# First layer of the expert tiles in transposed form, from a per-tile copy of the expert's weights

## What is computed

```
logits = LN(x) @ router_W + router_b          # [128, 64, 8]
top1 = argmax(softmax(logits)); gate = softmax(logits)[top1]
h = relu(LN(x) @ W1[e] + b1[e])               # W1[e]: 128 x 512, e = top1
y = h @ W2[e] + b2[e]                         # W2[e]: 512 x 128
x = x + gate * y
```

## Time and profile before

| | us |
|---|---|
| median of 3 runs | 1803.63 (1802.99 to 1806.22) |
| the profiled execution, its own time | 1804.93 |
| span of its profile | 1803.2 |
| stage of the tiles, first weight load to the last instruction | 1599.5 to 1803.2 |
| of that, first to 70th `output` (69 periods) | 182.41 |

### The profile page before, as it was taken

How to read it: one execution, slowest core, us unless ns; L and a number is a source line. 1 busy time by engine, 2 the same in 40 slices (tenths; PEclk the granted TensorE clock), 3 DMA queues, 4 the chain that set the end, 5 groups by cost and what they waited for, 6 DMA issues and landing times. The chain is left out here.

```text
span 1803.2 us, 82779 instructions
## 1 busy us (share of the span) xinstructions
PE 1479.9 (82%) x34347; PEld 1289.7 (72%) x34348; DVE 1159.9 (64%) x4481; ACT 736.0 (41%) x1856; POOL 220.0 (12%) x427
## 2 busy tenths in 40 slices
PE   1547777777756999999999999999999968249997
PEld 0436666666645888888888888888888858237665
DVE  5878888888875666565656566666666658425454
ACT  2436666665643344444434343434443422013332
POOL 0000000000000000000000000000000003743333
PEclk9868988888966999999999999999999975569999
DMA  6000000000030000000000000000000036322221
GB/s 222 1 1 1 0 0 0 0 0 0 0 84 12 1 0 0 0 0 0 0 0 0 0 0 0 0 0 0 0 0 0 0 103 208 128 84 75 75 75 42
DMA packets 33458, 50.04 MB, mean 28 GB/s; under 512 B 4714, under 2 KB 24684, under 8 KB 32648
## 3 DMA queue, kind: packets, MB, share of 16 engines
q1 hardware_dynamic: 27312, 35.50, 6.7%
q0 software_dynamic: 5376, 12.66, 2.0%
q10 hardware_dynamic: 728, 1.34, 0.2%
HBM read 30.52 MB, written 19.48 MB: 28 GB/s over the span
## 5 line engine op out<-in xcount | busy, mean ns | idle before, releaser
L1554 DVE TENSOR_TENSOR hb<-psH,b_sb 128x512 f32<-128x512 f32 x72 | 49.8, 692 | 118.4 <-PE psH L1349 118.4
L891 PE MATMUL sc_a<-h_a,KH 128*128 128x48 f16 (+2 forms) x4096 | 123.9, 183 | 2.5 <-DVE h_a L1045 2.5
L891 PE MATMUL sc_b<-h_b,KH 128*128 128x48 f16 (+2 forms) x4096 | 122.9, 183 | 0.0
L851 PE MATMUL z_a<-h_a,WL 128*128 128x64 f16 x2304 | 112.5, 193 | 9.3 <-DVE h_a L1037 1.9
L851 PE MATMUL z_b<-h_b,WL 128*128 128x64 f16 x2304 | 111.9, 193 | 8.4 <-DVE h_b L1037 0.6
L931 PEld LDWEIGHTS mx_b<-pmv_b,VH 128*128 128x128 f16 x4096 | 107.1, 96 | 16.4 <-DVE pmv_b L1073 16.4
L931 PEld LDWEIGHTS mx_a<-pmv_a,VH 128*128 128x128 f16 x4096 | 107.1, 96 | 16.2 <-DVE pmv_a L1073 16.2
L931 PE MATMUL mx_b<-pmv_b,VH 128*128 128x16 f16 x4096 | 113.0, 169 | 5.4 <-DVE pmv_b L1073 0.4
L931 PE MATMUL mx_a<-pmv_a,VH 128*128 128x16 f16 x4096 | 113.0, 169 | 5.2 <-DVE pmv_a L1073 0.4
L891 PEld LDWEIGHTS sc_a<-h_a,KH 128*128 128x128 f16 x4096 | 112.8, 96 | 2.8 <-DVE h_a L1045 2.6
L466 PE MATMUL psK<-ident,xn 128*128 128x128 f32 x64 | 20.9, 327 | 113.2 <-DVE VB L671 86.6
(11 more groups left out here) (291 smaller groups left out, 3556.6 us busy)
## 6 DMA issues: line engine op xcount, KB each, us to landing
xr<-sorted_x SPq DMA_DIRECT2D x72, 129.0 KB, 2.1
XT<-in_ctxT SPq DMA_DIRECT2D x1, 4096.0 KB, 13.2
x_scratch<-X SPq DMA_DIRECT2D x1, 4096.0 KB, 15.9
TOK<-x_scratch SPq DMA_DIRECT2D x4, 1024.0 KB, 10.6
sorted_x<-zt SPq DMA_DIRECT2D x16, 129.0 KB, 6.4
w_sb<-in_w SPq DMA_DIRECT2D x1, 2048.0 KB, 10.3
b_sb<-in_b SPq DMA_DIRECT2D x1, 2048.0 KB, 21.1
out<-ys,xr POOLq DMA_INDIRECT x72, 2.3
```

The source lines that it names most:

```text
L851: mm = nc.tensor.matmul(q.z[layer][:, j * GB:(j + 1) * GB], WL[:, blk + j, w, :], mov[m], start=False, stop=False, skip_group_check=True)
L891: mm = nc.tensor.matmul(A.S[:, WIDE * n:WIDE * n + streamed(n)], KH[:, k, pair * P:(pair + 1) * P], A.h[1][:, 2 * n:2 * n + streamed(n) // ...
L1554: nc.vector.tensor_tensor(hb[:, u, :], psH[:, u, :], b1_sb[:, bass.ds(col, FF)], ALU.add).then_inc(v_hb, 1)
```

## The change

The first layer is computed transposed: `hidden` now takes blocks of 128 columns of the expert's `W1` as the stationary operand and streams `xgT` past them, so that the result is hidden units x tokens, which is what `output` needs. The transposes (`turn_hidden`) and `hb` are gone. The four blocks go two to `psH`, two to `psHT`, with a semaphore each (`p_h`, `p_h2`). As the bias is now one value per partition, bias and ReLU are one operation per block: ACT does blocks 0 and 1 from `psH`, DVE blocks 2 and 3 from `psHT`. The stationary operand is read from `w1_e`, which DVE fills per tile with a copy of the expert's 512 columns (`weights`). The bias comes from a small array `b1T`, 128 x 32, transposed on the host.

```diff
-                    def hidden(j, u, col):
+                    def hidden(j, u):
                         pe.wait_ge(a_xt, j + 1)
-                        wait(pe, v_hb, j - 1)
-                        nc.tensor.matmul(psH[:, u, :], xgT[:, u, :], w1_sb[:, bass.ds(col, FF)],
-                                         start=True, stop=True).then_inc(p_h, 1)
-
-                    def turn_hidden(j, u):
-                        ...
+                        pe.wait_ge(v_w1, j + 1)
+                        wait(pe, a_ht, 2 * (j - 1))
+                        wait(pe, v_ht, 2 * (j - 1))
+                        for c in range(FC):
+                            h = (psH, psHT)[c // 2]
+                            mm = nc.tensor.matmul(h[:, u, c % 2 * P:(c % 2 + 1) * P], w1_e[:, u, c * P:(c + 1) * P], xgT[:, u, :],
+                                                  start=True, stop=True)
+                            if c % 2 == 1:
+                                mm.then_inc((p_h, p_h2)[c // 2], 1)
 
                     def output(j, u, col):
-                        pe.wait_ge(a_ht, j + 1)
+                        pe.wait_ge(a_ht, 2 * j + 2)
+                        pe.wait_ge(v_ht, 2 * j + 2)
...
                     def step(j, u8):    # TensorE
+                        if tile(j + 2):
+                            turn(j + 2, (u8 + 2) % RING)
                         if tile(j + 1):
-                            next_col = first_column(j + 1)
+                            hidden(j + 1, 1 - u)
                         if tile(j - 1):
                             before_col = first_column(j - 1)
-                        if tile(j + 2):
-                            turn(j + 2, (u8 + 2) % RING)
-                        if tile(j):
-                            turn_hidden(j, u)
-                        if tile(j + 1):
-                            hidden(j + 1, 1 - u, next_col)
                         if tile(j - 1):
                             output(j - 1, 1 - u, before_col)
...
                     def relu(j, u):     # ACT
-                        act.wait_ge(p_ht, j + 1)
+                        col = act.value_load(etab[0:1, 2, bass.ds(j, 1)], min_val=0, max_val=(NE - 1) * FC)
                         wait(act, p_y, j - 1)
-                        nc.scalar.activation(hT[:, u, :, :].rearrange("p c n -> p (c n)"), psHT[:, u, :],
-                                             ACT.Relu).then_inc(a_ht, 1)
+                        act.wait_ge(p_h, j + 1)
+                        for c in (0, 1):
+                            nc.scalar.activation(hT[:, u, c, :], psH[:, u, c * P:(c + 1) * P], ACT.Relu,
+                                                 bias=b1_sb[:, bass.ds(col + c, 1)]).then_inc(a_ht, 1)
...
                     def step(j, u8):    # ACT
                         if tile(j + 2):
                             turned(j + 2, u)
-                        if tile(j):
-                            relu(j, u)
+                        if tile(j + 1):
+                            relu(j + 1, 1 - u)
...
-                    def add_b1(j, u):
+                    def weights(j, u):  # DVE
                         col = dve.value_load(etab[0:1, 0, bass.ds(j, 1)], min_val=0, max_val=(NE - 1) * FF)
-                        ...
+                        wait(dve, p_h2, j - 1)
+                        nc.vector.tensor_copy(w1_e[:, u, :], w1_sb[:, bass.ds(col, FF)]).then_inc(v_w1, 1)
+
+                    def relu(j, u):     # DVE
+                        col = dve.value_load(etab[0:1, 2, bass.ds(j, 1)], min_val=0, max_val=(NE - 1) * FC)
+                        wait(dve, p_y, j - 1)
+                        dve.wait_ge(p_h2, j + 1)
+                        for c in (2, 3):
+                            nc.vector.tensor_scalar(hT[:, u, c, :], psHT[:, u, (c - 2) * P:(c - 1) * P],
+                                                    b1_sb[:, bass.ds(col + c, 1)], 0.0, ALU.add, ALU.max).then_inc(v_ht, 1)
...
                     def tile_step(j, u8):   # DVE
                         u = u8 % 2
                         if tile(j + 1):
-                            add_b1(j + 1, 1 - u)
+                            relu(j + 1, 1 - u)
+                        if tile(j + 2):
+                            weights(j + 2, u)
                         if tile(j - 1):
                             add_b2(j - 1, 1 - u)
                             finish(j - 1, (u8 + RING - 1) % RING)
```

More of the change, by code:

```diff
@@ L48, in decoder_kernel @@
 def decoder_kernel(nc, x, ctxT, wqT, wkT, wvT, wi0T, wh0T, bi0, bh0, wi1T, wh1T, bi1, bh1,
-                   xwq, woT, bo, rw, rb, w1, b1, w2, b2, out):
+                   xwq, woT, bo, rw, rb, w1, b1T, w2, b2, out):
     x1_dram = nc.dram_tensor("x1_scratch", [B, T, D], F32, kind="Internal").ap()
@@ L1113, in decoder_kernel @@
             w2_sb = sb("w2_sb", [P, NE * FC * D])
-            b1_sb = sb("b1_sb", [P, NE * FF])
+            b1_sb = sb("b1_sb", [P, NE * FC])
             b2_sb = sb("b2_sb", [P, NE * D])
@@ L1144, in decoder_kernel @@
             rowf = sb("rowf", [P, NT])
-            etab = sb("etab", [P, 2, NT], I32)
+            etab = sb("etab", [P, 3, NT], I32)
             rtab = sb("rtab", [P, NT], I32)
@@ L1152, in decoder_kernel @@
             xgT = sb("xgT", [P, 2, P])
-            hb = sb("hb", [P, 2, FF])
+            w1_e = sb("w1_e", [P, 2, FF])
             hT = sb("hT", [P, 2, FC, P])
@@ L1191, in decoder_kernel @@
             p_h = sem("p_h")
-            v_hb = sem("v_hb")
-            p_ht = sem("p_ht")
+            v_ht = sem("v_ht")
+            p_h2 = sem("p_h2")
+            v_w1 = sem("v_w1")
             a_ht = sem("a_ht")
@@ L1229, in _ @@
                                    w2.rearrange("e (c p) n -> p e c n", p=P)).then_inc(s_wf, 16)
-                    sync.dma_start(b1_sb[:, :], b1.rearrange("(a e) f -> a (e f)", a=1).broadcast_to([P, NE * FF])).then_inc(s_wf, 16)
+                    sync.dma_start(b1_sb[:, :], b1T).then_inc(s_wf, 16)
                     sync.dma_start(b2_sb[:, :], b2.rearrange("(a e) f -> a (e f)", a=1).broadcast_to([P, NE * D])).then_inc(s_wf, 16)
@@ L1344, in first_column @@
                         return pe.value_load(etab[0:1, 0, bass.ds(j, 1)], min_val=0, max_val=(NE - 1) * FF)
-                    def hidden(j, u, col):
+                    def hidden(j, u):
                         pe.wait_ge(a_xt, j + 1)
-                        wait(pe, v_hb, j - 1)
-                        nc.tensor.matmul(psH[:, u, :], xgT[:, u, :], w1_sb[:, bass.ds(col, FF)],
-                                         start=True, stop=True).then_inc(p_h, 1)
-                    def turn_hidden(j, u):
-                        pe.wait_ge(v_hb, j + 1)
-                        wait(pe, a_ht, j - 1)
-                        for c in range(FC):
-                            mm = nc.tensor.transpose(psHT[:, u, c * P:(c + 1) * P], hb[:, u, c * P:(c + 1) * P], ident[:, :])
-                        mm.then_inc(p_ht, 1)
+                        pe.wait_ge(v_w1, j + 1)
+                        wait(pe, a_ht, 2 * (j - 1))
+                        wait(pe, v_ht, 2 * (j - 1))
+                        for c in range(FC):
+                            h = (psH, psHT)[c // 2]
[3 more added lines that the diff above has]
+                                mm.then_inc((p_h, p_h2)[c // 2], 1)
                     def output(j, u, col):
-                        pe.wait_ge(a_ht, j + 1)
+                        pe.wait_ge(a_ht, 2 * j + 2)
+                        pe.wait_ge(v_ht, 2 * j + 2)
                         wait(pe, v_yb, j - 1)
@@ L1368, in _ @@
                     turn(0, 0)
-                    hidden(0, 0, first_column(0))
+                    hidden(0, 0)
                     turn(1, 1)
@@ L1407, in turned @@
                         act.wait_ge(p_xt, j + 1)
-                        wait(act, p_h, j - 1)
+                        wait(act, p_h2, j - 1)
                         nc.scalar.activation(xgT[:, u, :], psX[:, u, 0:P], ACT.Copy).then_inc(a_xt, 1)
                     def relu(j, u):
-                        act.wait_ge(p_ht, j + 1)
+                        col = act.value_load(etab[0:1, 2, bass.ds(j, 1)], min_val=0, max_val=(NE - 1) * FC)
                         wait(act, p_y, j - 1)
-                        nc.scalar.activation(hT[:, u, :, :].rearrange("p c n -> p (c n)"), psHT[:, u, :],
-                                             ACT.Relu).then_inc(a_ht, 1)
+                        act.wait_ge(p_h, j + 1)
+                        for c in (0, 1):
+                            nc.scalar.activation(hT[:, u, c, :], psH[:, u, c * P:(c + 1) * P], ACT.Relu,
+                                                 bias=b1_sb[:, bass.ds(col + c, 1)]).then_inc(a_ht, 1)
                     turned(0, 0)
                     turned(1, 1)
+                    relu(0, 0)
                     def step(j, u8):
@@ L1527, in tables @@
```

(14 more changed lines are left out.)

## The result

The changed kernel takes 1972.3 us in the median of four runs (1971.6 to 1973.4) against 1804.5 us of the kernel before: a ratio of 1.093, interval 1.0911 to 1.0949. It is slower by 168 us, where 88 were forecast, and outside the range of 1842 to 1945. Experiment 4 has a further measurement of the changed kernel, with its own runs of before beside it: 1.0928 (1.091 to 1.0946).

A forecast was written before the change was run, and what follows sets the result against it. TensorE was taken to bound the kernel before; the change would close a loop whose seven terms sum to 3.93 us a period against 2.644, over 69 periods +88.7 us, giving 1892 us, range 1842 to 1945.

The forecast's parts named there:

- the loop: In the tiles, each period runs output, DVE's two ReLUs, weights copy, hidden, output in sequence: 3.93 us against 2.644.
- end to ReLU: From the end of output's last matmul to DVE's start on the ReLU: 0.14 us.
- ReLU to copy: On DVE, first ReLU to the copy's start, with a table read in the queue: 0.90 us, between 0.45 and 1.2.
- term 6: TensorE's queue reads the table between hidden and output, leaving a gap of 0.35 us, between 0 and 0.6.
- term 4: From DVE's end of the copy to TensorE's first weight load for hidden: 0.10 us, between 0.05 and 0.20.
- terms 5 and 7: TensorE's matmuls: hidden 0.96 us from first load, and output 1.05 us to the end of its last matmul.
- the clock falls: Rival: TensorE's pauses drop its clock to 1.2 GHz; 1939 us if half the periods, 1985 throughout; chance 17%.
- The shared port: Rival: DVE's copy waits for POOL's DMA issue of 0.98 us each period, giving 4.91 and 1960 us; chance 6%.
- The gain without the loop: On TensorE, removing 0.45 us of transposes a tile would gain up to 31 us if nothing else changed.
- TensorE faster: Rival: copy is in place before output ends, TensorE stays the bound, period 2.26 us, time 1777; chance 5%.
- no change: Rival: time ends within 0.2% of before, the period landing between 2.59 and 2.70 us; chance 2%.
- a sign of being wrong: Wrong if TensorE has no idle time before psH, or if ACT releases it; DVE's w1_e was expected, about 100 us.

The follow-up runs named there:

- Experiment 4: Changed kernel with four, two or one idle identity products before hidden's wait for the copy, two ReLU waits moved forward: 1.0535, 1.0523, 1.0524 against the kernel before.
- 1: Changed kernel with DVE's copy of the weights (weights(j+2)) put in front of relu(j+1): 1.0187 against the kernel before.
- 2: Changed kernel with four buffers of hT instead of two, queue order kept, so ReLU waits for output of three tiles back: 1.0162 against the kernel before.
- 6: Changed kernel, steps written out, weights copied twice 1.0531, three times 1.1162, twice with one idle product 1.0546, against the kernel before.
- experiment 5: Steps written out in place of the program's loop: changed kernel 1.0405, kernel before 0.9915, experiment 3 0.9735, each against the kernel before.
- experiment 3: Changed kernel with the weights copy in front and all four ReLU blocks on ACT: 0.9821 against the kernel before; with steps written out 0.9735, 1757.95 us.
- control: The kernel before, with its tile steps written out in place of the program's loop: 0.9915 against the kernel before.

## Why the prediction was wrong, point by point

**What bounds the kernel, and the loop: right.** TensorE was the bound. The new orders close a loop over `output`, ReLU, copy and `hidden`, at the place named. Two independent edits that open it (1, 2) take the time to within 2% of before, and the doubled copy shows up in full (6).

**The terms at 2.4 GHz: right in sum.** The forecast was 3.93 us a period and +88.7 us. With the clock held by one product, the measured difference is 0.0524 x 1805 = +95 us, and about 106 with the 0.20 us that the moved waits had saved: more than the sum, and inside its ends of +30 and +151. Term by term, forecast, then the period at 1607, then the loop (experiment 4, four products, where `output` ends at 1702.19): end to ReLU 0.14, 0.15, 0.24; ReLU to copy 0.90, 0.89, 0.98; copy 0.43, 0.43, 0.43; copy to first load 0.10, 0.06, 0.11; `hidden` with the queue's gap and `output` 2.36, 2.21, 2.27. Sums 3.93, 3.74, 4.03. The gap of term 6 was put too high: from `hidden`'s first load to `output` it was 1.00 to 1.06 us in the written-out steps, where 1.31 was forecast, and `output` itself took 1.15 for 1.05. The register work of the loop was in no term. For the changed kernel itself term 4 was 0.32 in the loop, beyond its upper end of 0.20.

**The clock: the step that failed.** "The likeliest gives 1892" took terms 5 and 7 at 2.4 GHz. The rival "the clock falls" had 17%, at 1939 if it held in half the periods and 1985 throughout. It is what happened: 56 of the 69 periods ran at 0.64 in the mean and at 5.37 us each (1655.60 to 1956.16). About 60 us of the 168 are the clock: 56 x (5.37 - 4.25), with the estimate of experiment 4. That the rival's 5.28 lies so near 5.37 is partly luck: 5.28 was worked out for a period wholly at 1.2 GHz, and two periods that were so (1676.39 to 1688.36, granted 0.51 and 0.50) took 6.22 and 5.75; the mean is lower because the clock came back in between. The chance was too small. The earlier trace rows showed one pause that was followed by a fall and one that was not, and I let that stand for a small chance, though the new kernel repeats its pause 69 times. The same trace had more to say: from 250 to 507 us TensorE pauses 24 times for 1.8 to 1.9 us, and 16 of these pauses were followed by a fall to 1.2 GHz within 2 us of their end. The Trainium skill ("TensorE: Matmul & The Clock Gate", section A second HAM failure mode: psum-queue depth-cycling), whose rule had been cited for the rival, describes a clock that goes back and forth where the engine idles between groups; the trace agrees, with 0.64 granted.

**What lets it fall** is shown in direction, not as a rule. Against the change, the clock held when the pause was made shorter by a product and the moved waits (4), and all but held when the steps were written out (5). In written-out steps it fell more often the longer the pause was: two long periods with one copy, ten with two, nearly all with three (6). The traces can be read once more for this. The table counts TensorE's pauses in the tiles that are over 1 us long and begin and end at 2.4 GHz, and those of them with a fall within 2 us of their end, in the profiled execution of each version:

| version | pauses | length, us | followed by a fall |
|---|---|---|---|
| changed kernel, written-out steps | 12 | 1.45 to 1.83 | 0 |
| changed kernel, loop | 25 | 1.64 to 2.01 | 23 |
| one product, loop | 57 | 1.24 to 1.82, all but one under 1.6 | 0 |
| all written out, one copy | 68 | 1.45 to 1.84, 64 under 1.6 | 1, after 1.82 |
| all written out, two copies | 65 | 1.80 to 2.20 | 5 |
| the same with a product | 66 | 1.61 to 2.10 | 2, after 1.98 and 2.09 |
| all written out, three copies | 23 | 2.14 to 2.16 | 23 |

No pause under 1.6 us in the tiles was followed by a fall, in these or in any other version here. The forecast took the pause as about 1.5 us, which it is in the written-out steps (1.47 mostly); in the loop it grew to 1.6 to 2.0. So the register work of the loop, small in itself, took the pause from a length that never cost the clock here to one that can. What stays open is what decides between 1.6 and 2.2 us: in the loop almost every such pause was followed by a fall, in written-out steps with two copies 5 of 65. Length alone does not explain that, and no run here shows what does.

**The shared port: rightly left out.** The copy took 427 ns in the mean of 67 (the groups by line above), never beside POOL's issue. In experiment 1, 65 of the 70 copies after 1600 us overlap an issue of POOL in time, and none took longer than 429 ns. In experiment 2, 58 of 70 do, and here they took longer, but by little (experiment 1 first, then 2):

```profile
L1554 DVE COPY w_e<-w_sb x72: 426/427/429, 1596.9 to 1837.6; 128x512 f32 x72
...
L1554 DVE COPY w_e<-w_sb x72: 426/462/675, 1578.9 to 1841.0; 128x512 f32 x72
```

(minimum, median, maximum in ns). By the Trainium skill ("SBUF — State Buffer", section Who interferes with whom) a copy in a two-port mode shares a port with GpSimd, and whoever comes second waits until the other's instruction has ended, which could be up to POOL's 0.98 us for a copy (an estimate from that rule and the row of 0.98). The traces do not agree: the worst case in these rows lost 0.25 us. Why only experiment 2 lost anything was not tried.

**The gain without the loop: right.** 69 x 0.45 = 31 us was the bound for the transposes. Written out on both sides (experiment 5, same chip), experiment 3 is 1758.0 us against the control's 0.9915 x 1805.5 = 1790.1: 32 us.

**TensorE faster, or no change:** did not occur. The profile names ACT's `xgT` as the releaser of `hidden` for 27 of 118 us, which the prediction had as a sign of being wrong; in the periods shown above and at 1654 `xgT` had ended half a microsecond before the copy did.

## What to carry to other kernels

For each wait in front of an instruction in a queue, ask what stands behind it and who needs that next: a copy that could have run at any time cost (1.0928 - 1.0187) x 1805 = 134 us here, clock included, because a ReLU that waits for a buffer stands in front of it. One swap of two calls, or two more buffers, undoes most of it. Count too what stands behind the last wait: two waits left there, with a threshold that the loop computes, made the load 0.20 us later. And once a change makes TensorE pause in every period, look up every pause of that length in the trace of before, price its matmuls at 1.2 GHz too and give that case its due chance; here 0.4 us less in the pause took 1.3 us off the period (5.37 to 4.05).

## What the runs showed that was not expected

- Register work in a loop of the program is not free: the same steps take 2.43 us written out and 2.61 in the loop before the change, 1.93 and 2.19 in experiment 3, 3.65 and 4.05 in experiment 4.
- A matmul product with no use, 0.21 us in each period, with two waits moved in front of it, made the kernel 73 us faster; about 60 of these are the clock.
- A second copy of 0.43 us in each period (1.0531) left the written-out kernel faster than the loop with one (1.0928).
